# Perceiver block in 13 units a batch: the last 64 context tokens and the 64 latents share one unit, the token left over is handled by itself

## The reference, cut to what matters

```
x: (16, 64, 128) latents, ctx: (16, 1601, 128) context tokens
# cross attention, 16 heads of 64, each of 16 batches:
l = layer_norm(norm(x)); c = layer_norm(ctx)
q = l @ Wq;  k, v = split(concat([c, l]) @ Wkv)      # 1601 + 64 keys
x = x + softmax(q k^T / 8) v @ Wo                    # 64 queries x 16 heads = 1024 columns
# then a differential self attention over 64 latents and a top-2 mixture of 8 experts
x = x + self_attention(norm(x)); x = x + experts(norm(x))
```

## Time and profile before

| | us |
|---|---|
| median of 3 runs (all: 1000.93, 997.82, 996.78) | 997.82 |
| the profiled execution, its own time | 998.82 |
| its span, first to last instruction | 997.1 |
| mean granted TensorE clock | 0.974 |

### The profile page before, as it was taken

The page is one execution under the profiler, slowest core; times in us unless marked ns, Lnnn a source line. Parts: engine busy times, 40 slices in busy tenths (PEclk is TensorE's granted clock), DMA queues, the critical chain, the costliest instruction groups (busy, mean ns, idle before and its releaser), DMA issues.

```text
span 997.1 us, 19671 instructions
## 1 busy us (share of the span) xinstructions
PE 944.7 (95%) x7942; PEld 501.6 (50%) x7942; DVE 782.8 (79%) x1540; ACT 738.6 (74%) x1017; POOL 376.0 (38%) x376
## 2 busy tenths in 40 slices
PE   8679999999999999999999999999999998969975
PEld 5434455454545454545454545454545454547742
DVE  5968796969696969696969696969695956658965
ACT  4576878787878787878787878787878776635631
POOL 6471143433333343434343434343434223143343
PEclk9799999999999999999999999999999999979987
DMA  6212020302020312121212121121212000000000
GB/s 204 68 22 58 11 79 15 76 17 74 18 73 18 73 17 73 23 68 25 66 24 67 23 68 33 59 37 54 32 48 35 22 2 22 1 23 23 2 7 16
DMA packets 73218, 41.79 MB, mean 42 GB/s; under 512 B 60932, under 2 KB 68520, under 8 KB 73128
## 3 DMA queue, kind: packets, MB, share of 16 engines
q1 hardware_dynamic: 72840, 39.49, 16.4%
q10 hardware_dynamic: 288, 1.05, 0.3%
HBM read 25.98 MB, written 0.59 MB: 27 GB/s over the span
## 4 chain that ended last, share of the span: by engine, by line
PE 81%; DVE 13%; ACT 2%; issue 2%; POOL 1%; DMA 1%; POOLq 0%; ACTq 0%; DVEq 0%
PE S L1977 10%; PE S L1985 9%; PE S L1979 9%; PE OA L2006 9%; PE OA L2008 9%; PE OA L2010 9%; PE WW L1942 8%; PE WW L1958 1%; PE WW L1960 1%; DVE mx L1417 1%; PE WW L1959 1%; PE WW L1929 1%; DVE amx L720 1%; PE WW L1931 1%; PE WW L1930 1%
## 5 line engine op out<-in xcount | busy, mean ns | idle before, releaser
L1429 DVE TENSOR_TENSOR region<-S,region 128x1024 f16<-128x1024 f32 (+1 forms) x224 | 272.1, 1215 | 107.5 <-ACT S L1726 106.8
L1721 ACT ACTIVATE region<-S,sigma 128x1024 f16<-128x1024 f32 (+1 forms) x224 | 250.3, 1117 | 121.4 <-PE S L1985 121.4
L1417 DVE TENSOR_REDUCE mx<-WW 128x1 f32<-128x512 f32 (+1 forms) x480 | 263.6, 585 | 29.9 <-PE WW L1942 21.2
L1726 ACT ACTIVATE S<-S,sigma 128x1024 f32<-128x1024 f32 (+1 forms) x224 | 244.1, 1090 | 0.0
L1977 PE MATMUL S<-region,xT_hi 128*128 128x512 f16 (+1 forms) x416 | 124.3, 380 | 3.4 <-DVE region L1429 2.2
L2006 PE MATMUL OA<-region,xk 128*128 128x512 f16 (+1 forms) x416 | 124.4, 381 | 0.0
L1985 PE MATMUL S<-region,xT_lo 128*128 128x512 f16 (+1 forms) x416 | 124.2, 380 | 0.0
L2008 PE MATMUL OA<-region,xk 128*128 128x512 f16 (+1 forms) x416 | 124.2, 380 | 0.0
L1979 PE MATMUL S<-region,xT_hi 128*128 128x512 f16 (+1 forms) x416 | 124.1, 380 | 0.0
L2010 PE MATMUL OA<-region,xk 128*128 128x512 f16 (+1 forms) x416 | 124.0, 380 | 0.0
L1942 PE MATMUL WW<-xT_hi,region 128*128 128x512 f16 x360 | 120.3, 380 | 1.6 <-DVE region L1408 0.9
(11 more groups left out here) (296 smaller groups left out, 1728.3 us busy)
## 6 DMA issues: line engine op xcount, KB each, us to landing
raw<-ctx SPq DMA_DIRECT2D x16, 768.0 KB
rb<-inv_dram SPq DMA_DIRECT2D x16, 512.0 KB, 3.6
raw<-ctx SPq DMA_DIRECT2D x16, 32.5 KB
WO_lo<-L_xattn_Wq ACTq DMA_DIRECT2D x1, 512.0 KB, 3.9
WO_hi<-L_xattn_Wkv ACTq DMA_DIRECT2D x1, 512.0 KB, 4.8
lx<-x SPq DMA_DIRECT2D x1, 512.0 KB, 5.9
region<-L_xattn_Wo SPq DMA_DIRECT2D x1, 512.0 KB, 8.0
WO_hi<-L_xattn_Wkv SPq DMA_DIRECT2D x1, 512.0 KB, 8.9
```

What stands on the lines that cost most here:

```text
L1417: nc.vector.tensor_reduce(mx[:, r, c:c + 1], W[BANK[("m", n)]][:, 0:width], AX.X, ALU.max)\
L1429: nc.vector.tensor_tensor(p_lo[k][0:r, :], src, p_hi[k][0:r, :], ALU.subtract)\
L1721: nc.scalar.activation(p_hi[k][0:r, :], src, ACT.Exp, scale=sigma[0:r, 0:1])
L1726: nc.scalar.activation(src, src, ACT.Exp, scale=sigma[0:r, 0:1]).then_inc(e_done.sem, 1)
```

## The change

A batch has 13 units. The last, `LAT` = 12, holds 64 of the 65 tokens of the last tile (`KEPT`) on partitions 0 to 63 and the 64 latents on partitions 64 to 127. Its scores are issued in pairs, tokens then latents, with weights of 64 columns to the two halves of one bank's partitions; its weighing in pairs too, tokens from rows 0 to 63 into OA, latents from rows 64 to 127 into WW. The last weighing into OA is therefore the merged one, which stands behind the scores of unit 1 of the next batch (`weigh(old, LAT - 1 + u)`), and `outputs` waits for it, at the same place in ScalarE's program as before.

The token left over (number 1600, `LEFT`) goes by itself: "lf", a late item of unit 2, makes its 1024 scores with 16 matmuls of 2 or 1 columns; VectorE sums them (128 x 8), ScalarE takes two exponentials of 128 x 8 in unit 3, VectorE their difference in unit 4, "lt", a late item of unit 5, transposes them by one matmul with weights of 16 columns, ScalarE copies the result, three transfers lay it out as three rows of 1024, and `weigh_left` adds it to OA in unit 10 by two matmuls of 3 rows. Two small transfers bring the token's own values.

The maxima are spread over units 3 to 11 instead of 3 to 12. GpSimd copies the latents' halves to partitions 64 to 127, after the split of the tokens. In the last batch three steps that prepare the tail stand one unit earlier, and two waits and one semaphore guard the banks.

```diff
@@ -27,8 +27,11 @@
...
-UNITS = TILES + 1
-LAT = TILES
+UNITS = TILES
+LAT = TILES - 1
+KEPT = REST - 1
+LEFT = FULL * 128 + KEPT
+assert KEPT + NQ == 128
...
@@ -85,17 +88,16 @@
...
-        ([], []),
-        ([("q", 0), ("q", 1)], some(0, 1)),
-        (some(1, 2), some(3, 2)),
-        ([("q", 2), ("q", 3)], some(5, 1)),
-        (some(6, 2), some(8, 2)),
-        (some(10, 2), some(12, 2)),
-        (some(14, 2), some(16, 1)),
-        (some(17, 2), some(19, 2)),
-        (some(21, 2), some(23, 1)),
-        (some(24, 2), some(26, 2)),
-        (some(28, 2), some(30, 2)),
+        ([], [("lf", 0)]),
+        ([("q", 0), ("q", 1)], some(0, 2)),
+        (some(2, 2), some(4, 2)),
+        ([("q", 2), ("q", 3)], some(6, 1) + [("lt", 0)]),
+        (some(7, 2), some(9, 2)),
+        (some(11, 2), some(13, 2)),
+        (some(15, 2), some(17, 2)),
+        (some(19, 2), some(21, 2)),
+        (some(23, 2), some(25, 2)),
+        (some(27, 2), some(29, 3)),
...
@@ -111,14 +113,17 @@
...
-NORMALISE_AT = {6: [0], 7: [1, 2], 8: [3, 4, 5], 9: [6], 10: [7], 11: [8, 9], 12: [10, 11], 13: [12]}
+NORMALISE_AT = {6: [0], 7: [1, 2, 3], 8: [4, 5, 6], 9: [7, 8, 9], 10: [10, 11], 11: [12]}
...
+LEFT_EXP_AT, LEFT_LOW_AT, LEFT_AT = 3, 4, 10
...
@@ -439,6 +458,23 @@
...
+        def left_columns(sp, turn):
+            p = turn.off % 2
+            if turn.off >= 2:
+                sp.wait_ge(pv_done.sem, pv_done.upto(turn.plus(-2), LEFT_AT - 1))
+            sp.dma_start(left_x[p][0:2, :], xk[p][KEPT:REST, :, FULL, :]).then_inc(left_x_in[p].sem, 16)
+            sp.dma_start(left_x[p][2:3, :], xk_hi[p][KEPT:REST, FULL, :]).then_inc(left_x_in[p].sem, 16)
+        def left_rows(sp, turn):
+            sp.wait_ge(free["lt"].sem, free["lt"].upto(turn))
+            if turn.off > 0:
+                sp.wait_ge(pv_done.sem, pv_done.upto(turn.plus(-1), LEFT_AT - 1))
+            for k, first in enumerate((0, 0, 8)):
+                sp.dma_start(left_row[k:k + 1, :].rearrange("o (r n) -> o r n", n=128), left_pT[first:first + 8, :])\
+                  .then_inc(left_row_in.sem, 16)
         def inverse_rows(sp, turn):
...
@@ -1239,19 +1276,22 @@
...
+            left_columns(sp, Turn(0))
...
-                sp.dma_start(lk_odd[k][:], lk[k][NQ:128]).then_inc(ld_lk.sem, 16)
+                sp.dma_start(lk_even[k][NQ:128], lk[k][0:NQ]).then_inc(ld_lk.sem, 16)
...
+                    left_columns(sp, Turn(b + 1))
...
+                left_rows(sp, Turn(b))
...
@@ -1423,11 +1463,20 @@
...
+            def left_scores(turn):
+                dve.wait_ge(pe_item["lf"].sem, pe_item["lf"].upto(turn))
+                parts = W[BANK[("lf", 0)]][:, 0:32].rearrange("p (r c) -> p r c", c=4)[:, :, 0:3]
+                nc.vector.tensor_reduce(left_s[:], parts, AX.X, ALU.add).then_inc(free["lf"].sem, 1)
+            def left_low_part(turn):
+                dve.wait_ge(left_exp.sem, left_exp.upto(turn))
+                nc.vector.tensor_tensor(left_p[:, 8:16], left_e[:], left_p[:, 0:8], ALU.subtract)\
+                  .then_inc(left_low.sem, 1)
...
@@ -1439,6 +1488,10 @@
...
                         if kind == "m" and prep:
...
+                        if kind == "lf":
+                            left_scores(b)
+                    if u == LEFT_LOW_AT:
+                        left_low_part(b)
...
@@ -1559,15 +1612,19 @@
...
-                if turn.off == 1:
+                if turn.off == 0:
...
-                nc.gpsimd.tensor_copy(ck_hi[p][:], at_batch(0, turn))
-                nc.gpsimd.tensor_copy(ck_lo[p][:], at_batch(1, turn)).then_inc(curk.sem, 1)
+                pool.wait_ge(split.sem, split.upto(turn if turn.off else Turn(1), GROUPS - 1))
+                nc.gpsimd.tensor_copy(ck_hi[p][NQ:128], at_batch(0, turn))
+                nc.gpsimd.tensor_copy(ck_lo[p][NQ:128], at_batch(1, turn)).then_inc(curk.sem, 1)
+                pool.wait_ge(curk.sem, curk.upto(turn))
...
+                    if b.off == 0:
+                        current_k(b)
...
@@ -1713,20 +1769,30 @@
...
+            def left_exponentials(turn):
+                act.wait_ge(free["lf"].sem, free["lf"].upto(turn))
+                nc.scalar.activation(left_p[:, 0:8], left_s[:], ACT.Exp, scale=sigma[:, 0:1])
+                nc.scalar.activation(left_e[:], left_s[:], ACT.Exp, scale=sigma[:, 0:1]).then_inc(left_exp.sem, 1)
+            def left_turned(turn):
+                act.wait_ge(pe_item["lt"].sem, pe_item["lt"].upto(turn))
+                if turn.off > 0:
+                    act.wait_ge(left_row_in.sem, turn.times(48))
+                nc.scalar.copy(left_pT[:], W[BANK[("lt", 0)]][0:16, 0:128]).then_inc(free["lt"].sem, 1)
             def outputs(turn):
-                act.wait_ge(pv_done.sem, pv_done.upto(turn, TILES - 1))
+                act.wait_ge(pv_done.sem, pv_done.upto(turn, LAT))
...
@@ -1761,6 +1827,8 @@
...
+                    if u == LEFT_EXP_AT:
+                        left_exponentials(b)
...
                     if u == 0 and post:
                         outputs(old)
...
@@ -1770,6 +1838,8 @@
...
+                        if item[0] == "lt":
+                            left_turned(b)
...
@@ -1944,6 +2014,17 @@
...
+                if kind == "lf":
+                    for r in range(8):
+                        rows = slice(128 * r, 128 * r + 128)
+                        mm(w[:, 4 * r:4 * r + 2], q_hi[p][:, rows], xT[p][:, :, LEFT], start=True, stop=True)
+                        ins = mm(w[:, 4 * r + 2:4 * r + 3], q_lo[p][:, rows], xT_hi[p][:, LEFT:LEFT + 1],
+                                 start=True, stop=True)
+                if kind == "lt":
+                    pe.wait_ge(left_low.sem, left_low.upto(turn))
+                    if turn is LAST:
+                        pe.wait_ge(x1_read.sem, 1)
+                    ins = mm(w[0:16, 0:128], left_p[:], ident16[:], start=True, stop=True)
                 if kind == "mt":
...
@@ -1961,63 +2042,87 @@
...
             def scores(turn, u):
...
+                    keys_of = [(slice(0, KEPT), xT_hi[p][:, at], xT_lo[p][:, at], 0),
+                               (slice(KEPT, 128), cT_hi[p][:], cT_lo[p][:], COLS)]
...
-                    mm(score_bank(u, k)[0:r], hi, q_hi[p][:, cols[k]], start=True, stop=False)
+                    for r, hi, lo, qc in keys_of:
+                        mm(banks[r, k, :], hi, q_hi[p][:, cols(qc, k)], start=True, stop=False)
...
             def weigh(turn, u):
...
+                    tok, own = slice(0, KEPT), slice(KEPT, 128)
+                    parts = [(tok, xk_hi[p][tok, u, :], xk_lo[p][tok, u, :], outs, first, last),
+                             (own, ck_hi[p][own], ck_lo[p][own], [W[BANK[("ol", k)]] for k in range(2)], True, True)]
...
-                    mm(dst[k], hi, ph[0:r, cols[k]], start=first, stop=False)
+                    for r, hi, lo, dst, first, last in parts:
+                        mm(dst[k], hi, ph[r, cols[k]], start=first, stop=False)
...
+            def weigh_left(turn):
+                pe.wait_ge(left_x_in[turn.off % 2].sem, raw_loaded(turn))
+                pe.wait_ge(left_row_in.sem, turn.times(48, 48))
+                for k in range(2):
+                    mm(OA[:, k, :], left_x[turn.off % 2][:], left_row[:, HALF * k:HALF * k + HALF],
+                       start=False, stop=False)
@@ -2028,17 +2133,19 @@
...
-                    elif post and u == 0:
-                        weigh(old, TILES - 1)
-                    elif post and u == LATENTS_AT:
-                        weigh(old, LAT)
+                    elif post:
+                        weigh(old, LAT - 1 + u)
+                    if u == LEFT_AT:
+                        weigh_left(b)
...
+                        pe.wait_ge(free["lf"].sem, free["lf"].upto(LAST))
...
+                        pe.wait_ge(free["lt"].sem, free["lt"].upto(LAST))
```

More of the change, by code:

```diff
@@ L183, in perceiver @@
         lk = [sb(f"lk{k}", [128, TB, D], F16) for k in range(2)]
-        lk_odd = [sb(f"lk_odd{k}", [NQ, TB, D], F16) for k in range(2)]
+        lk_even = [sb(f"lk_even{k}", [128, TB, D], F16) for k in range(2)]
         lT_hi = sb("lT_hi", [128, B * NQ], F16)
@@ L189, in perceiver @@
         cT_lo = [sb(f"cT_lo{p}", [128, NQ], F16) for p in range(2)]
[L190 to L191 removed]
+        ck_hi = [sb(f"ck_hi{p}", [128, D], F16) for p in range(2)]
+        ck_lo = [sb(f"ck_lo{p}", [128, D], F16) for p in range(2)]
         raw = [sb(f"raw{p}", [128, TILES, D]) for p in range(2)]
@@ L302, in perceiver @@
         free = {"q": sem("q_lo_done", 4), "m": sem("m_reduced", MAXIMA, 1),
-                "mt": sem("m_row", 2), "ol": sem("ol_copied", 2), "pj": sem("pj_copied", 1)}
+                "mt": sem("m_row", 2), "ol": sem("ol_copied", 2), "pj": sem("pj_copied", 1),
+                "lf": sem("left_summed"), "lt": sem("left_turned")}
+        left_exp = sem("left_exp")
+        left_low = sem("left_low")
+        left_row_in = sem("left_row_in")
+        left_x_in = [sem(f"left_x_in{p}") for p in range(2)]
```

(24 more changed lines are left out.)

77 lines of the change are left out of this document (44 added, 33 removed).

## The result

The changed kernel takes **1018.44 us** (1017.08 to 1022.71), the kernel before 997.81 (996.78 to 1000.93) on the same chip: ratio 1.0225, 95% interval 1.0187 to 1.0262. It is slower by 20.6 us where 16.4 were predicted. The profiled execution took 1017.08, its span is 1015.3, TensorE's granted clock 0.974.

A forecast was written before the change was run, and what follows sets the result against it. TensorE, busy 49.48 of 49.53 us, was taken to bound: 49.53 - 2.59 + 1.36 = 48.30, 47.95 without old waits, plus 1.38 and 1.41 gives 50.74 a batch. In all +16.4: 1015.2 profiled, 1014 median, range 1003 to 1026.

The forecast's parts named there:

- The pairs run together: On TensorE, the 13th token tile's 12 matmuls run beside the latents' matmuls, taking 2.59 us off a batch.
- The additions: On TensorE, "lf" 0.46, "lt" 0.25 and `weigh_left` 0.65 add 1.36 us a batch.
- The first wait: Ahead of unit 3's scores, ScalarE's copy of OA waits for the merged weighing, costing TensorE 1.38 us a batch.
- The banks: In units 3, 4, 5, 7 and 11 TensorE waits for banks of WW: 1.41 us a batch, 0.35 before.
- The batch: One full batch takes 50.74 us, 1.21 us more than before.
- The ends: First batch -0.2 to -0.5 us; last batch 0, with -1 to 2.
- the gain stands: Rival, chance 0.07: ScalarE makes up its 2.0 before unit 3, banks cost as before; 980 us.
- Only the first wait: Rival, chance 0.13: 1.38 comes, banks cost 0 to 0.3 a batch; 995 to 1000 us, no change that can be told.
- The clock: Rival, chance 0.05: TensorE's clock falls in each new pause, 21 us on top; 1036 us.
- the pairs did not run one after another: Denies a rival, chance 0.04: merged pairs run serially on TensorE, 2.59 us come back each batch; 1055 us.

The follow-up runs named there:

- e6: The changed kernel without anything for the left-over token (its matmuls, steps and transfers), the pairs kept: 1001.21 us, ratio 1.0042.
- e1: The kernel before, unmerged, with one edit: ScalarE's copy of OA waits for the latents' weighing: 1021.37 us, ratio 1.0265.
- e2: The changed kernel with ScalarE's copy of OA behind both exponentials of unit 1 instead of in front: 1002.45 us, ratio 1.0082.
- e8: The changed kernel with the merged weighing in unit 0, directly behind the other old weighing: 1005.74 us, ratio 1.0094.
- e4: The changed kernel with VectorE taking each maximum over 64 columns only, TensorE's instructions unchanged: 1007.93 us, ratio 1.013.
- e10: The changed kernel with the edits of e2 and e7's paired short maxima and their placement, nothing moved to VectorE: 993.58 us, ratio 0.997.
- e3: The changed kernel with the copy of OA on VectorE, ahead of unit 1's low part, unit 1's statistics behind it: 1011.58 us, ratio 1.0165.
- e5: e3 with the copy directly behind unit 0's low part, ahead of the casts; statistics and last two casts behind unit 1's low part: 1013.84 us, ratio 1.0179.
- e7: e5 with short maxima two to a bank and reduction, one maximum in unit 3, "lt" in unit 4: 1004.29 us, ratio 1.0072.
- e9: e7 with VectorE's queue in units 1 and 2 re-ordered, the left-over scores' sum ahead of casts and statistics: 998.66 us, ratio 1.0014.

## Why the prediction was right

**The pairs run together: right.** 0.22 from pair to pair (the rows of 422.71 and 463.13), within 0.01 inside one, on partitions and on columns. The rule in the Trainium skill, "TensorE: Matmul & The Clock Gate", Part 3, that weight loads overlap only across row groups, would have lengthened the steps of the merged scores. The trace differs: with weights of their own, pairs that share all rows start 0.22 apart, as full matmuls do.

**The additions: right.** "lf" takes 0.40 (427.80 to 428.19), not 0.46; matmuls of one or two columns follow each other by 0.025. `weigh_left` takes 0.62 for 0.65. "lt" and `weigh_left` together were put at 0.90; e6 gives 1.04 with the waits around them.

**The first wait: right, place, chain and size.** Copy of OA 5.49 (5.50 predicted), "lf" at 9.07 (9.04), low part 8.53 (8.55), scores of unit 3 at 9.81 (9.82). Unit 2 lasts 4.43, of which 2.60 and "lf"'s 0.40 are matmuls: 1.43 of wait for 1.38. e1 shows the cause by itself: 1.83 without "lf" as cover, 1.43 with its 0.40. e2 and e8 give 0.95 and 0.81 a batch back by changing only what queues behind the copy, or when it may start.

**The banks: right in sum, near in place.** 1.41 predicted: 0.31, 0.08, 0.31, 0.44, 0.27 in units 3, 4, 5, 7, 11. In unit 3, 4.79 stand against 4.21 and one maximum more (0.22): 0.36. In unit 4 e4 takes away 0.07, in unit 7 0.45. For unit 5, e6 leaves 4.21 without "lt", so "lt" with its wait is 0.58, and less its 0.25 the wait is 0.33. In unit 11 the matmul stands at 43.62, where 43.61 was forecast, 0.55 behind the one before it where full matmuls follow by 0.22: 0.33. In sum 1.54. e4 shows that reductions carry only half of it (0.76).

For unit 3 the working had the times right (casts from 12.36, forecast 12.39; conversion done at 14.32, forecast 14.29), but the cause only in part. It took the wait for an echo of the late copy through ScalarE's queue. In e2 that queue is no longer behind and 0.26 of the 0.36 is still there, while e10, with one maximum in the unit instead of two, has none. Most of it is the second maximum, put on the bank of queries that are still to be cast and converted.

**The batch: 50.74 predicted, 50.89 measured.**

**The ends: near by luck.** The first batch gained 1.8 where 0.2 to 0.5 were forecast, and 1.7 of that is the granted clock (rows at 71.30); at the same clock it would have gained about 0.1. The last lost 1.1, inside its -1 to 2, but there too a stretch at 0.50 that the kernel before has the earlier trace rows is absent: seven small matmuls and the six of the next scores take 2.1 us instead of 3.5. Whether the shorter pause ahead of it (2.4 for 3.3) brought that isn't shown. At the clock of before the last would have lost about 2.5, outside its range, and both ends together would have added an estimated 2.4 (the sum of -0.7, 1.7 and 1.4) instead of the forecast -0.5. As it was, together they give -0.7, and the 14 full batches 18.9 for 16.9, so the profiled execution came to 1017.08 for 1015.2. The other 2.5 of the distance from 1014 to 1018.4 is the step to the median: I kept it 1 us under the profiled time, as before the change, and this time it lies 1.4 above; why the other executions took longer isn't shown.

**Missed: VectorE's casts** wait for the merged weighing as last reader of their buffer. It cost nothing in the changed kernel and 0.73 a batch in e3 (unit 2 lasts 3.92 there and 3.19 in e5, where the copy goes ahead of the casts).

**The rivals.** The premise of "the gain stands" was wrong: ScalarE can't make up time it spends idle in front of the waiting copy. "Only the first wait" failed by the banks, which cost as much again. The clock stayed at 1.00 in the batch in spite of pauses of 0.92 us, and the pairs did not run one after another.

## What to carry to other kernels

When two products are merged, every reader of either waits for both: list the waits on the old semaphores (here ScalarE's copy and VectorE's casts), and look at what queues in order behind each, since that, not the reader, is what reaches the bounding engine. Taking 2.6 us off an engine that is busy 49.48 of 49.53, with 1.3 added again, made the kernel slower. With one step on ScalarE moved behind two others (e2) and the maxima in pairs as well (e10), it only came back to 0.3% under its old time. A freed wait is worth what stands until the next one: e3, e5, e7 and e9 each took one away and met the next within a unit or two.

## What the hardware showed beside it

A cast of 508 columns on VectorE takes 0.42 us alone. In e5 the first of the two casts in the row at 426.57 takes 1.35 (the second, of 127 columns, 0.21). It starts inside the second of these two subtractions of GpSimd:

```profile
425.26 2.37 POOL L1604 TENSOR_TENSOR xk<-raw,xk 128x508 f16<-128x508 f32 x2 [10.70 <-DVE xk L1342]
```

In the full batches of e2, e5, e7, e9 and e10 a cast that starts inside such a subtraction, with 0.49 us or more of it left, ends 0.28 to 0.29 us behind the subtraction's end every time. With 0.49 us left it lasts 0.77 (e2 and e10), with 0.66 left 0.94 (once, in e9), with 1.06 left 1.35 (e5 and e7). The other way round, a subtraction that starts inside a cast lasts 1.26 instead of 1.15. So the cast behaves as if it waited for the end of the subtraction. VectorE's low part (1.22) and its statistics (0.20 from one to the next) beside GpSimd kept their lengths. An order of steps on VectorE that looks free can cost 0.9 us in this way. It is read from the overlap of the rows, and no run took GpSimd's step away.
